# Head outputs of the first twelve batches through DRAM instead of through TensorE turns

## The reference

```python
x = x + 0.5 * ffn(layernorm(x))     # rows quantized in blocks of 32 to a 6-bit grid, then a 128x128 product
x = x + attention(layernorm(x))     # 16 heads of 8 features
x = x + 0.5 * ffn(layernorm(x))

# attention, for each batch and head
scores = (Q @ K.T) / sqrt(8) + 0.3 * log(mask_h + 1e-6)     # 512x512; the mask is that of the head
out_h  = softmax(scores) @ V_h                              # 512x8
result = concat(out_h over 16 heads) @ Wo + bo
```

## Time and profile before

| | |
|---|---|
| median of three executions | 877.73 us (876.89 to 878.03) |
| the profiled execution | 877.97 us |
| its span in the profile | 876.0 us |
| mean granted TensorE clock | 0.948 of full |
| start of head 2 | 158.87 us |
| copy of head 62's output, behind the last exponential of head 63 | 829.89 us |

### The profile page before, as it was taken

How to read it: one execution, slowest core, us unless ns; L and a number is a source line. 1 busy time by engine, 2 the same in 40 slices (tenths; PEclk the granted TensorE clock), 3 DMA queues, 4 the chain that set the end, 5 groups by cost and what they waited for, 6 DMA issues and landing times.

```text
span 876.0 us, 13047 instructions
## 1 busy us (share of the span) xinstructions
PE 738.6 (84%) x4355; PEld 259.7 (30%) x4355; DVE 556.2 (63%) x1464; ACT 669.2 (76%) x799; POOL 191.0 (22%) x164
## 2 busy tenths in 40 slices
PE   0376626999999999999999999999999998999844
PEld 0043311232333323333333234223321331331234
DVE  8866573866889756899784456885433457432265
ACT  1379654888888788888888888888888887888811
POOL 0305750202353203163240031341200002000011
PEclk9987755999999999999999999999999999999987
DMA  5529497865666674756867538668676555456101
GB/s 148 121 77 370 174 314 248 254 209 160 200 207 198 196 222 138 221 185 165 248 191 231 180 114 234 204 170 247 200 225 186 173 173 173 150 192 208 42 1 53
DMA packets 56071, 162.11 MB, mean 185 GB/s; under 512 B 14121, under 2 KB 24497, under 8 KB 45579
## 3 DMA queue, kind: packets, MB, share of 16 engines
q1 hardware_dynamic: 51740, 154.36, 57.4%
q0 software_dynamic: 1808, 5.94, 2.1%
q10 hardware_dynamic: 2446, 0.89, 0.5%
HBM read 117.87 MB, written 43.29 MB: 184 GB/s over the span
## 4 chain that ended last, share of the span: by engine, by line
PE 53%; DVE 20%; ACT 10%; issue 8%; DMA 6%; POOL 2%; SPq 1%; ACTq 0%; DVEq 0%; POOLq 0%
PE S_PS L1614 19%; PE O_PS L1628 18%; ACT BIG L738 9%; DVE S_PS L1212 5%; PE F_PS L1515 4%; PE R_PS L1637 3%; PE F_PS L1510 2%; DMA PART<-trig_parts 2%; DMA k_parts<-PART 2%; PE P_PS L1552 1%; DVE PART L1114 1%; PE P_PS L1515 1%; DVE SC L1053 1%; DVE XC L1098 1%; DVE BIG L1043 1%
## 5 line engine op out<-in xcount | busy, mean ns | idle before, releaser
L738 ACT ACTIVATE BIG<-S_PS 128x1024 f32<-128x1024 f32 x512 | 508.5, 1023 | 109.9 <-PE S_PS L1614 107.6
L1614 PE MATMUL S_PS<-BIG 98*128 98x512 bf16 x1024 | 311.3, 389 | 37.4 <-DMA BIG<-shift_rows 13.7
L1212 DVE COPY S_PS<-BIG 128x512 f32<-128x512 f32 x256 | 159.6, 687 | 180.7 <-ACT BIG L738 178.5
L1628 PE MATMUL O_PS<-BIG,VX 128*9 128x512 f32 x2048 | 268.4, 597 | 1.2 <-ACT OTS L747 1.2
L1614 PEld LDWEIGHTS S_PS<-BIG 98*128 98x128 bf16 x1024 | 79.2, 98 | 290.7 <-ACT BIG L738 136.1
L572 POOL TENSOR_TENSOR XDT<-PART 128x512 bf16<-128x512 f32 x24 | 28.8, 1201 | 292.9 <-ACT PART L706 292.9
L1628 PEld LDWEIGHTS O_PS<-BIG,VX 128*9 128x9 f32 x2048 | 30.8, 88 | 103.4 <-issue 98.7
L549 POOL TENSOR_TENSOR X<-X,BFH 128x512 f32<-128x512 f32 x16 | 24.0, 1521 | 155.2 <-DVE BIG L1043 120.2
L588 POOL TENSOR_TENSOR PART<-PART 128x512 bf16<-128x512 f32 x32 | 41.5, 1297 | 38.5 <-DVE PART L1120 38.5
L581 POOL TENSOR_TENSOR PART<-PART 128x512 f32<-128x512 f32 x32 | 39.6, 1239 | 42.6 <-DVE PART L1114 41.2
L779 ACT ACTIVATE BIG<-S_PS,TEMP 128x1024 f32<-128x1024 f32 x32 | 34.4, 1111 | 18.1 <-PE S_PS L1801 17.6
(11 more groups left out here) (190 smaller groups left out, 737.8 us busy)
## 6 DMA issues: line engine op xcount, KB each, us to landing
BIG<-ln_masks SPq DMA_DIRECT2D x62, 1024.0 KB, 6.3
ln_masks<-BIG SPq DMA_DIRECT2D x16, 1024.0 KB, 7.1
BIG<-q_parts SPq DMA_DIRECT2D x63, 192.0 KB
BIG<-k_parts SPq DMA_DIRECT2D x63, 144.0 KB
BIG<-q_parts SPq DMA_DIRECT2D x63, 128.0 KB
q_parts<-PART SPq DMA_DIRECT2D x9, 768.0 KB, 3.8
k_parts<-PART SPq DMA_DIRECT2D x18, 384.0 KB, 4.7
BIG<-k_parts SPq DMA_DIRECT2D x63, 96.0 KB
```

Source lines behind the costliest of these rows:

```text
L738: act.activation(E[:, m % 2, j, 2 * pair:2 * pair + 2, :], S_PS[:, pair, :, :], ACT.Exp, scale=LOG_WEIGHT)\
L1212: ve.tensor_copy(S_PS[:, pair, i, :], LNM[:, slot, 2 * pair + i, :]).then_inc(s["seeded"], 1)
L1614: mm = pe.matmul(S_PS[:, pair, i, :], KT[0:ALL_ROWS, slot, K_COL[j], 128 * kb:128 * kb + 128], QT[0:ALL_ROWS, slot, j, :], start=False, st ...
L1628: mm = pe.matmul(O_PS[32 * j:32 * j + HD + 1, :], VX[:, slot_of(n), j, kb, h, :], E[:, m % 2, j, kb, :], start=kb == 0, stop=kb == T - 1)
```

## The change

The heads of the first three rounds (`FIRST_TURNED = 48` heads, `BY_DRAM = 3` rounds) are no longer turned. SyncE stores `OTS` whole to DRAM by head. In the next round, at head 2, it loads the sums of all heads of the round as one tile of 128 x 256, VectorE inverts them in one instruction, SyncE stores the inverses (head 3) and loads them back broadcast over the eight features of each head (head 4), and loads the outputs as `ROWS`, features on partitions. Four products of 128 x 512 normalize them, and `ROWS` is what `out_product` takes, so `turn_at` and `at_copy` go too. Round 3 keeps the old way. `R_PS` is no longer shared with the turns in rounds 0 to 2, so waits between the turns and the bounds are gone. The tables of ticks are changed along with it.

```diff
+BY_DRAM = NQ - 1
+FIRST_TURNED = NH * BY_DRAM
 LATE  (round 0, first half)   turn_pe=(82, 90), xd_copy_act=(82, 90), ffn_pe=(84, 92)   -> (81, 89), (81, 89), (84, 92)
 LATE  (round 0, second half)  turn_pe=(110, 118), xd_copy_act=..., ffn_pe=(112, 120)    -> (113, 121), ..., (114, 122)
 LATE  (round 1, first half)   reduce_ve=34, scales_ve=36, to_grid_ve=41, from_grid_ve=44, turn_pe=(50, 58), ffn_pe=(52, 60)
                                                                 -> 41, 42, 49, 50, (65, 73), (66, 74)
 LATE  (round 1, second half)  turn_pe=(110, 118), ffn_pe=(112, 120)                     -> (113, 121), (114, 122)
-CHAINS = ((43, 59, 75, 91), (3, 27, 51, 75), (3, 27, 51, 75), ())
-APART = dict(norm_ve=-2, turn_pe=0, xnt_act=1, q_pe=5, q_act=5, ...
+CHAINS = ((43, 59, 75, 91), (11, 35, 59, 83), (11, 35, 59, 83), ())
+APART = dict(norm_ve=-7, turn_pe=-2, xnt_act=-2, q_pe=5, q_act=5, ...
-AMID = dict(turn_pe=(10, 18, 26, 34), at_act=(10, 18, 26, 34), out_pe=(12, 20, 28, 36), add_ve=(13, 21, 29, 37),
-            stats_ve=(16, 24, 32, 40), lnexp_act=42, centre_ve=49, rstd_ve=50, reduce_ve=56, scales_ve=58,
-            to_grid_ve=64, from_grid_ve=72, turn_xd_pe=(75, 82, 90, 98), ffn_pe=(77, 84, 92, 100), ...
+SUMS_HEAD = 2
+AMID = dict(invert_ve=20, normalize_ve=(36, 38, 44, 46), out_pe=(42, 44, 50, 52), add_ve=(43, 45, 51, 53),
+            stats_ve=(44, 48, 52, 56), lnexp_act=58, centre_ve=59, rstd_ve=60, reduce_ve=64, scales_ve=66,
+            to_grid_ve=67, from_grid_ve=72, turn_xd_pe=(82, 89, 97, 105), ffn_pe=(84, 90, 98, 106), ...
-ALONE = dict(turn_pe=(14, 22, 30, 38), at_act=(14, 22, 30, 38), out_pe=(16, 24, 32, 40), ...
-             turn_xd_pe=(62, 70, 78, 86), xd_copy_act=(62, 70, 78, 86), ffn_pe=(64, 72, 80, 88), ...
+ALONE = dict(invert_ve=20, normalize_ve=(36, 38, 40, 42), out_pe=(40, 42, 48, 50), ...
+             turn_xd_pe=(73, 81, 89, 97), xd_copy_act=(73, 81, 89, 97), ffn_pe=(74, 82, 90, 98), ...
...
+            def store_o(m):
+                n, h = m // NH, head_of(m)
+                sp.wait_ge(s["o_copied"], m + 1)
+                if n >= 2:
+                    sp.wait_ge(s["rows_in"], 16 * (n - 1))
+                sp.dma_start(O_D[n % 2, h].rearrange("r j l -> j r l"), OTS[:, :]).then_inc(s["o_out"], 16)
+
+            def load_sums(n):
+                sp.wait_ge(s["o_out"], 16 * NH * (n + 1))
...
+                sp.dma_start(SUMS[:, 0, :],
+                             O_D[n % 2, :, HD].rearrange("h j (q x) -> h (j q) x", x=SUMS.shape[2]))\
+                  .then_inc(s["sums_in"], 16)
+                sp.dma_start(ROWS.rearrange("p j l -> p (j l)"),
+                             O_D[n % 2, :, 0:HD].rearrange("h d j l -> h d (j l)")).then_inc(s["rows_in"], 16)
+
+            def store_inverses(n):
+                sp.wait_ge(s["inverted"], n + 1)
...
+            def load_inverses(n):
+                sp.wait_ge(s["inverse_out"], 16 * (n + 1))
+                sp.dma_start(INV.rearrange("p j l -> p (j l)"),
+                             INV_D.rearrange("h j l -> h (j l)")[:, None, :].to_broadcast((NH, HD, QB * L)))\
+                  .then_inc(s["inverse_in"], 16)
@@ head(m), behind load_mask(m + 1) and ahead of load_stack(m + 1)
+                if 2 <= m < FIRST_TURNED + 2:
+                    store_o(m - 2)
+                if q > 0:
+                    if i == SUMS_HEAD:
+                        load_sums(q - 1)
+                    if i == SUMS_HEAD + 1:
+                        store_inverses(q - 1)
+                    if i == SUMS_HEAD + 2:
+                        load_inverses(q - 1)
@@ o_copy(m)
-                    act.wait_ge(s["o_turned"], m)
+                if m > FIRST_TURNED:
+                    act.wait_ge(s["o_turned"], m - FIRST_TURNED)
+                elif past(m):
+                    act.wait_ge(s["o_out"], 16 * m)
@@ VectorE
+            def invert(n):
+                ve.wait_ge(s["sums_in"], 16 * (n + 1))
+                ve.reciprocal(SUMS[:, 1, :], SUMS[:, 0, :]).then_inc(s["inverted"], 1)
+
+            def normalize(n, j):
+                ve.wait_ge(s["rows_in"], 16 * (n + 1))
+                ve.wait_ge(s["inverse_in"], 16 * (n + 1))
+                TT(ROWS[:, j, :], ROWS[:, j, :], INV[:, j, :], ALU.mult).then_inc(s["at_ready"], 1)
...
-                    if k == 1 and m >= 2:
+                    if k == 1 and m >= FIRST_TURNED + 2:
                         o_norm(m - 2)
@@ TensorE
+            def out_product(n, j):
+                g = n * QB + j
+                if n < BY_DRAM:
+                    pe.wait_ge(s["at_ready"], g + 1)
...
+                    rows_product(epilogue_bank(n, j), ROWS[:, j, :], WO, "y_psum")
...
-                    if k == 1 and m >= 2:
-
-                        c = CHAINS[q]
-                        done = len([a for a in c if a + SECOND[q]["norms_q_pe"] <= tick])
-                        turned = len([a for a in c if a + SECOND[q]["turn_bound_pe"] <= tick])
-                        pe.wait_ge(s["bound_sq"], 3 * (1 + QB * q + done))
-                        pe.wait_ge(s["bound_copied"], 1 + QB * q + turned)
+                    if k == 1 and m >= FIRST_TURNED + 2:
                         turn_o(m - 2)
```

More of the change, by code:

```diff
@@ L89 @@
[L89 to L95, removed]
@@ L173, in macaron_kernel @@
         QT = big(30720, 2048).bitcast(BF16).rearrange("p (s c l) -> p s c l", s=2, c=4)
+        ROWS, INV = (big(20480 + 2048 * i, 2048).rearrange("p (j l) -> p j l", j=QB) for i in range(2))
+        SUMS = big(22528, 2 * QB * NH * L // 128).rearrange("p (i x) -> p i x", i=2)
         def stage(h):
@@ L284, in slot_of, with at_of, centred_of @@
             return n % 2 if is_short(n) else 0
+        def at_of(n):
+            return X[0] if n == BY_DRAM else AT[:, 0]
+        def centred_of(n):
+            return AT[:, 1] if n < BY_DRAM else at_of(n)
         def calls_of(n, k):
@@ L433, in head @@
                     load_mask(m + 1)
+                if 2 <= m < FIRST_TURNED + 2:
[7 more added lines that the diff above has]
+                        load_inverses(q - 1)
+                if more and m >= 1:
                     if m == 1:
@@ L820, in attention @@
                     if q > 0:
-                        if tick in LAST[q]["at_act"]:
-                            at_copy(q - 1, LAST[q]["at_act"].index(tick))
                         if tick == LAST[q]["lnexp_act"]:
@@ L1039, in centre @@
                     ve.wait_ge(s["xn_turned"], QB * (n - 1) + js.stop)
-                if f == 1:
-                    ve.wait_ge(s["at_turned"], QB * n + js.stop)
+                if f == 1 and n < BY_DRAM:
+                    ve.wait_ge(s["at_ready"], QB * (n + 1))
+                elif f == 1:
+                    ve.wait_ge(s["at_turned"], QB * (n - BY_DRAM) + js.stop)
                 rows = "p j t n -> p (j t) n"
@@ L1324, in background @@
                     n = q - 1
+                    if tick == LAST[q]["invert_ve"]:
+                        invert(n)
+                    if tick in LAST[q]["normalize_ve"]:
+                        normalize(n, LAST[q]["normalize_ve"].index(tick))
                     if tick in LAST[q]["add_ve"]:
@@ L1641, in turn_at @@
                 g = n * QB + j
-                pe.wait_ge(s["o_normed"], (n + 1) * NH)
-                if is_short(n) and n == NQ - 1:
+                pe.wait_ge(s["o_normed"], (n + 1) * NH - FIRST_TURNED)
+                if is_short(n):
                     if j >= 2:
@@ L1673, in turn_xd1 @@
                     pe.wait_ge(s["ffn_added1"], g)
-                turn(epilogue_bank(n, j), AT[:, slot_of(n), j, :, :], "xd_turned1")
+                turn(epilogue_bank(n, j), centred_of(n)[:, j, :, :], "xd_turned1")
             def ffn1(n, j):
@@ L1680, in background @@
             def background(q, tick):
-                m, k = q * NH + tick // STEPS, tick % STEPS
-                normed = max(m - 2 + (k > 1), 0)
                 if q == 0:
@@ L1711, in background @@
                     n = q - 1
-                    if tick in LAST[q]["turn_pe"]:
-                        turn_at(n, LAST[q]["turn_pe"].index(tick))
                     if tick in LAST[q]["out_pe"]:
@@ L1821, in _ @@
                 what(0, j)
-            norms_k(0, 0, 0)
+            norms_k(0, 0)
             norms_q(0, 0)
@@ L1832, in _ @@
                     t = t + 1
-                if what is norms_k:
-                    norms_k(0, j, 0)
-                else:
-                    what(0, j)
-            norms_k(0, 3, 0)
+                what(0, j)
+            norms_k(0, 3)
             norms_q(0, 3)
```

98 lines of the change are left out of this document (57 added, 41 removed).

## The result

The changed kernel took 1001.0 us (median of four, 989.5 to 1002.0) against 877.9 us for the kernel before in the same session: the ratio is 1.136, with a 95% interval of 1.132 to 1.140. It is 123 us slower. The forecast was 874.7 us with a range of 862 to 887.

A forecast was written before the change was run, and what follows sets the result against it. It took no engine alone as the bound, but a loop through TensorE, VectorE and ScalarE, with turns hidden in the seeding gap. Terms -4 - 2 - 6.5 + 5 - 2 + 2 + 2 + 2.5 = -3.0 gave 874.7 us, range 862 to 887.

The forecast's parts named there:

- The new transfers: Term for the head stores and new loads: stacks land in time, inverses about 1.2 us late in rounds 1 and 2; +2.5.
- a stack that lands behind the scores' start in most heads: Sign named in advance as making the forecast wrong: a head's loads landing after its scores should start, in most heads.
- The front's turn at tick 1: Two terms for moving the front's turn and copy earlier: -6.5 mainly in rounds 1 and 2, +5 in round 0.
- the hidden place of the old one: In rounds 1 and 2 the front's turn takes the old head turn's place in the seeding gap; part of the -6.5.
- The inverses: Head 4's 1 MB load, landing 8.5 to 9.5 us after its start; rival with late landing: 880 to 884, chance 0.22.
- FFN turns and products: Term for moved FFN ticks: eight cost about 0.45 us more each, eight others gain 0.2 each; +2, bounds -3 and +6.
- head 55 keeps its stall: Within VectorE's by-head term: head 55 keeps its old form, so TensorE's 3.09 us wait there stays.
- VectorE's new work: Term for the reciprocal of 256 and twelve products: seeds some 2 us late in head 6 of round 1; +2.
- The turns of heads: Term for 48 turns leaving TensorE: mostly hidden behind the seeding at heads' starts, so only -4, bounds 0 and -26.
- the bare head: Sign: heads without other work stay at 9.68 us; below 9.4 the reading of the seeding gap is wrong.
- VectorE's piece by head: Term for dropping VectorE's reciprocal and product by head: 26 us of work, only -2 won, bounds 0 and -6.
- the output turns: Term for dropping twelve output turns and copies, with two products now in one head: -2, bounds +2 and -8.

The follow-up runs named there:

- a2_wait: Kernel before, plus only SyncE's wait for the output copy of two heads earlier before it issues the next stack, nothing stored: 878.2 us, ratio 0.999.
- a1_flat: Changed kernel with each head's output stored as 128 rows in tile order instead of outermost size 4, the rows loaded in four transfers: 950.3 us, ratio 1.077.
- c3_both: Changed kernel with 128-row stores, plus the front's ticks put back and the inverses' load issued at the end of head 3: 907.3 us, ratio 1.032.

## Why the prediction was wrong, point by point

**The step that failed first** is "The new transfers": "48 stores of 256 KB (3.0 us to landing for one of that size)", "so they land in time", "DMA engines are busy 66 to 67% ... and get about 6% of a head more". The row of 3.0 us is of an output store with 128 rows outermost. The head's store has 4, and by itself takes 5.87 us on 4 engines; the mean share of 16 engines says nothing of these four. Put at nothing in a term of +2.5 that was all for the inverses, the store alone is +47 to +51 (926.8 against 879.4, and 1001.0 against 950.3). I said what would make the forecast wrong, "a stack that lands behind the scores' start in most heads"; it did so in 25 heads of the rounds, fewer than half; but no rival carried it and the range did not reach it. My argument about the later issue of the seven loads was right (`a2_wait`: no cost), and so was that of the copy's wait, for stores of 128 rows.

**The front's turn at tick 1** was to bring -6.5 in rounds 1 and 2 and cost +5 in round 0. Undoing it brings 30.6 us. In round 0 the waits were where I had put them, of the weight loads at 2.7 to 4.3 us in `a1_flat` instead of 1.6 to 3.3, and 16.7 us of it stayed in the heads where I had let 5 of 9.3 stay. In rounds 1 and 2 I read "the hidden place of the old one" and left out the wait for the copy of V, which is in the same tick there too. The six waits for it are 1.5 to 3.0 us each, and these two rounds cost 12.4 us by the openings of heads, with the wrong sign in the sum.

**The inverses** were named as the tight place and as a rival at 880 to 884. The wait was 10.2, 13.1 and 5.1 us in the changed kernel; 12.5 us for the three rounds, measured on `a1_flat`. That round 3's would "come in time" was wrong: 5.1 us there, and 8.6 in `a1_flat`. In the changed kernel the load landed 16.3 and 16.0 us after the start of heads 20 and 36, not 8.5 to 9.5: it was issued 2.7 us into the head and took 13.6 and 13.3 from there. With the flat store it still took 11.4 and 10.7, and issued ahead of the parts and the mask (`c3_both`) 7.7 and 9.7. The 4.4 us for 1 MB that the prediction set beside its term are by the Trainium skill, "DMA: Bandwidth & Descriptors", section "Anatomy of one DMA", a fit of transfers that GpSimd issues; these loads are SyncE's, and none of them came near it.

**FFN turns and products**: +2 predicted (bound +6), 13.3 measured. The mechanism was right, a product in the middle of a head delays the next step, but it was mis-sized: heads 57 to 60 took 10.79 us where I had about 10.5. I also wrote that head 55 keeps its stall. It did not: it fell from 13.76 to 9.39 us, and head 56 rose from 10.02 to 13.53 in the changed kernel. The stall moved by one head; why is not shown.

**VectorE's new work, and two output products in a head**: head 22, "head 6 of round 1", was to be 2 us longer and is 3.5 in `c3_both`, with a cause that I had not named: the second product waits for VectorE's sum of the first in the same bank (`c3_both`).

```profile
393.99 0.68 DVE L1311 TENSOR_TENSOR X<-F_PS,X 128x512 f32<-128x512 f32 x1
394.82 1.73 PE L1594 MATMUL F_PS<-WO,BIG 128*128 128x128 f32 x8 [2.36 <-DVE X L1311]
```

The wait is in the trace. That it makes the head's 3.5 us is argued, not shown: this edit was not undone by itself.

**The turns of heads, -4, and the bare head** held: bare heads stay at 9.68 us, and in `c3_both` heads 3, 9, 10, 11, 49, 50 and 52 are 0.3 to 0.6 us shorter, 3.0 in all. That reading, that the turns hide behind the seeds, was the prediction's main claim, and heads 46 to 48, bare heads which lost their turn and became no shorter, bear it out; the 26 us of TensorE's time that went were worth about 3 in these seven heads. What the turns are worth in heads with other work was not tried by itself, nor were the two terms of -2, VectorE's piece by head and the output turns.

**The account.** From 1001.0: the store's form 50.7, the front's ticks 30.6, the inverses 12.5, FFN ticks 13.3, together 107.1, each a difference of two medians, of kernels that were not all run in the same session. What is left, 894.0 against 878.6 us, lies by the openings mostly in heads 19 to 22, 35 to 38 and 51 to 56, which carry the sums, the rows, the inverses and the paired products, less some 3 us in heads 16 to 18 and as much in 32 to 34, which carry less than before. How those 15 us divide between the megabytes and the pairs stays open: the two attempts to move the megabytes moved the late stack. No version here beats the kernel before.

## What to carry to other kernels

Before a transfer is costed by its bytes, read the outermost size of both its sides: a store that lands in 2.0 us as 128 rows held four engines for more than half of a head of 9.7 us here, and the loads behind it were late, while the mean DMA share showed nothing. Time it alone and count its packets less its rows: in this case that was the number of engines. Read the same of the loads that must not be late. When a piece is moved to an earlier tick, list all semaphores that it waits on and the tick of each one's signal, not only that of its input; a signal in the same tick is a wait of the length of what that engine has in front of it.

## What the runs showed of the hardware

A store of 256 KB took 5.87, 3.98, 2.85 and 2.0 us for outermost sizes 4, 8, 16 and 128, with 4, 8, 16 and 16 small packets beside its 128 rows and 25%, 46%, 90% and 89% of the 16 engines busy in its middle; the third and the fourth differ by 0.8 us from issue to landing at the same count, for which no run here has the cause. In the loop, whose heads take about 10 us, size 8 cost 3.4 us in the whole program and size 4 cost 47. And in the stalled rounds 0 to 2 the mean granted clock of TensorE was 0.90 to 0.94 for 1.00 before, and over all rounds it was busy 17 us longer with 240 fewer matmuls: part of what a late transfer costs is paid behind it.
